# A decoder layer on one core: up and down units of its expert network in one line through all visits

## What is computed

```
x = layernorm(x + attention(x))              # 16 heads of 16, softmax, projections wq wk wv wo
x = layernorm(x + recurrence(x, ctx))        # a decaying scan over tokens, with exp(x) and exp(-x)
x = layernorm(x + experts(x))                # 8 experts, 256 -> 1024 -> 256, tanh GELU
```

```
h1  = gelu(x @ W1[e] + b1[e])
out = sum over e of gate[:, e] * (h1 @ W2[e] + b2[e])
```

## Time and profile before

| | |
|---|---|
| time, three executions | 1025.46, 1026.37, 1026.95 us (median 1026.37) |
| the profiled execution | 1025.53 us, span 1023.8 us |
| TensorE matmuls busy | 917.6 us (90%) |
| VectorE, ScalarE busy | 602.8 and 602.0 us (59% each) |
| GpSimd busy | 84.2 us (8%) |
| HBM traffic | 165 GB/s over the span |

### The profile page before, as it was taken

The page is one execution under the profiler, slowest core; times in us unless marked ns, Lnnn a source line. Parts: engine busy times, 40 slices in busy tenths (PEclk is TensorE's granted clock), DMA queues, the critical chain, the costliest instruction groups (busy, mean ns, idle before and its releaser), DMA issues.

```text
span 1023.8 us, 17885 instructions
## 1 busy us (share of the span) xinstructions
PE 917.6 (90%) x6672; PEld 824.0 (80%) x6672; DVE 602.8 (59%) x1254; ACT 602.0 (59%) x1017; POOL 84.2 (8%) x116
## 2 busy tenths in 40 slices
PE   4558697988799989999899989999899989999997
PEld 3457586778688879888788879888798888899997
DVE  6747667776565555565556645565556636333765
ACT  4437775666556655555556655555566645444685
POOL 3301001100020001100020001100011000000000
PEclk8667987999999999999999999999999999999999
DMA  6337879755554545454544455445454545565350
GB/s 208 102 126 258 278 251 316 255 198 179 172 168 142 157 140 173 128 173 135 160 150 150 139 167 156 150 149 158 134 167 128 164 141 158 175 195 155 118 171 11
DMA packets 143541, 170.33 MB, mean 166 GB/s; under 512 B 11080, under 2 KB 110688, under 8 KB 143456
## 3 DMA queue, kind: packets, MB, share of 16 engines
q1 hardware_dynamic: 143456, 169.19, 52.3%
HBM read 133.50 MB, written 35.65 MB: 165 GB/s over the span
## 4 chain that ended last, share of the span: by engine, by line
PE 72%; DVE 12%; ACT 11%; issue 3%; DMA 0%; POOL 0%; SPq 0%; POOLq 0%; ACTq 0%; DVEq 0%
PE up_ps L448 11%; PE up_ps L450 10%; PE up_ps L449 10%; PE down_ps L664 10%; PE down_ps L666 9%; PE down_ps L665 9%; ACT probs L717 2%; ACT L717 2%; DVE h_lo L830 2%; DVE pt_lo L905 2%; PE bank L487 2%; PE bank L448 2%; PE bank L470 1%; PE bank L450 1%; PE bank L449 1%
## 5 line engine op out<-in xcount | busy, mean ns | idle before, releaser
L768 ACT ACTIVATE h_all<-up_ps,b_all 128x512 f32<-128x512 f32 (+1 forms) x296 | 182.4, 631 | 344.3 <-PE up_ps L450 340.0
L664 PE MATMUL down_ps<-w_hi,h_hi 128*128 128x256 f32 x1024 | 300.6, 294 | 32.0 <-DVE h_lo L830 31.9
L665 PE MATMUL down_ps<-w_lo,h_hi 128*128 128x256 f32 x1024 | 292.3, 285 | 0.0
L666 PE MATMUL down_ps<-w_hi,h_lo 128*128 128x256 f32 x1024 | 292.3, 285 | 0.0
L830 DVE TENSOR_TENSOR h_lo<-h_all,h_hi 128x512 fp32r<-128x512 f32 x256 | 176.7, 692 | 191.8 <-ACT h_hi L759 190.7
L664 PEld LDWEIGHTS down_ps<-w_hi,h_hi 128*128 128x128 f32 x1024 | 198.0, 193 | 46.2 <-issue 32.4
L448 PE MATMUL up_ps<-x2t_hi,w_hi 128*128 128x512 f32 (+1 forms) x592 | 224.7, 380 | 0.9 <-DVE x2t_lo L830 0.9
L449 PE MATMUL up_ps<-x2t_lo,w_hi 128*128 128x512 f32 (+1 forms) x592 | 219.4, 371 | 0.0
L450 PE MATMUL up_ps<-x2t_hi,w_lo 128*128 128x512 f32 (+1 forms) x592 | 219.3, 370 | 0.0
L665 PEld LDWEIGHTS down_ps<-w_lo,h_hi 128*128 128x128 f32 x1024 | 198.6, 194 | 4.4
L666 PEld LDWEIGHTS down_ps<-w_hi,h_lo 128*128 128x128 f32 x1024 | 198.6, 194 | 0.0
(11 more groups left out here) (172 smaller groups left out, 1008.5 us busy)
## 6 DMA issues: line engine op xcount, KB each, us to landing
w_hi<-w_parts SPq DMA_DIRECT2D x192, 256.0 KB, 3.1
w_lo<-w_parts SPq DMA_DIRECT2D x192, 256.0 KB, 3.4
w_raw<-in_w_dram SPq DMA_DIRECT2D x104, 256.0 KB, 3.8
w_parts<-w_hi SPq DMA_DIRECT2D x64, 256.0 KB, 3.7
w_parts<-w_lo SPq DMA_DIRECT2D x64, 256.0 KB, 4.1
x_in<-in_x_dram SPq DMA_DIRECT2D x8, 256.0 KB, 3.8
ctx_sb<-in_ctx_dram SPq DMA_DIRECT2D x8, 256.0 KB, 4.3
out_dram<-acc SPq DMA_DIRECT2D x8, 256.0 KB, 2.4
```

What stands on the lines that cost most here:

```text
L664: nc.tensor.matmul(ps, hi, w2h[:, c, :], start=c == 0 and j == 0, stop=False, skip_group_check=True)
L665: nc.tensor.matmul(ps, hi, w2l[:, c, :], start=False, stop=False, skip_group_check=True)
L666: mm = nc.tensor.matmul(ps, lo, w2h[:, c, :], start=False, stop=c == FC - 1 and j == PAIR - 1, skip_group_check=True)
L768: a = nc.scalar.activation(h_all[:, unit % HALL, k * wide:(k + 1) * wide], up_ps[unit % 2][:, k * wide:(k + 1) * wide], ACT.Gelu_apprx_tan ...
```

## The change

The units are put in one line through all visits, by `plan()`. After each up unit comes the down unit three behind it; the first down unit of a visit comes one up unit later, together with the second. A two-pair visit's items (after another two-pair visit) are now

```diff
-    def items(n):
-
-        m = units(n)
-        order = [("U", u) for u in range(LAG)]
-        for u in range(LAG, m):
-            order += [("D", u - LAG), ("U", u)]
-        return order + [("D", u) for u in range(m - LAG, m)]
+    def plan():
+        ups = [(n, u) for n in range(VISITS) for u in range(units(n))]
+        lines, downs = [[] for _ in range(VISITS)], 0
+        for g, (n, u) in enumerate(ups):
+            lines[n].append(("U", n, u))
+            while downs + LAG + (ups[downs][1] == 0) <= g:
+                lines[n].append(("D",) + ups[downs])
+                downs += 1
+        return lines[:-1] + [lines[-1] + [("D",) + unit for unit in ups[downs:]]]
+
+    ITEMS = plan()
+    LINE = [item for line in ITEMS for item in line]
+    LAST_DOWN = [max(i for i, (kind, m, _) in enumerate(LINE) if kind == "D" and m == n) for n in range(VISITS)]
...
+    def up_before(i):
+
+        return [LINE[i - 1][1:]] if i > 0 and LINE[i - 1][0] == "U" else []
+
+    def ended(i):
+
+        return [(n, [p for p in range(NPAIR) if n == JOIN[p] + E - 1]) for n in range(VISITS - 1) if LAST_DOWN[n] == i]
...
             def down(n, u):
 
                 unit = FIRST_UNIT[n] + u
-                if u == 0 and n > 0:
-                    pe.wait_ge(added, EVACUATED[n])
...
                     for a in range(pairs):
+                        if c == 0 and n > 0 and a < len(active(n - 1)):
+                            pe.wait_ge(added, EVACUATED[n - 1] + PAIR * (a + 1))
...
             for n in range(VISITS):
-                order = items(n)
-                for k, (kind, u) in enumerate(order):
-                    if k > 0 and order[k - 1][0] == "U":
-                        hidden_hi(n, order[k - 1][1])
+                for k, (kind, visit, u) in enumerate(ITEMS[n]):
+                    for unit in up_before(FIRST_ITEM[n] + k):
+                        hidden_hi(*unit)
                     if kind == "U":
-                        hidden(n, u)
-                    if n == 0:
-                        for part in FIRST_ROUTE.get(k, []):
-                            route(0, part)
+                        hidden(visit, u)
+                    for part in FIRST_ROUTE.get(FIRST_ITEM[n] + k, []):
+                        route(0, part)
...
-                for k, (kind, u) in enumerate(order):
-                    if k == 0 and n > 0:
-                        add_expert(n - 1)
+                for k in range(len(ITEMS[n])):
+                    for done, left in ended(FIRST_ITEM[n] + k - 1):
+                        add_expert(done)
                         for p in left:
                             finish(p, 0)
-                    if k > 0 and order[k - 1][0] == "U":
-                        hidden_lo(n, order[k - 1][1])
...
+                    for unit in up_before(FIRST_ITEM[n] + k):
+                        hidden_lo(*unit)
...
-BEGIN = (None, 0, 40, 88, 152, 216, 280, 344, 408)
-LENGTH = (None, 40, 48, 64, 64, 64, 64, 64, 64)
+BEGIN = (None, 0, 36, 85, 149, 213, 277, 341, 405)
+LENGTH = (None, 36, 49, 64, 64, 64, 64, 64, 64)
...
-NORM3_ITEM, STORE_ITEM = 2, 4
...
+NORM3_AFTER, STORE_AFTER = 3, 5
+FIRST_PIECES = [(0, 0, 0), (0, 0, 1), (0, 0, 2), (0, 0, 3), (0, 1, 0), (0, 1, 1), (0, 1, 2)]
+FREE_FIRST = {0: [(0, 1, 3)], 1: [(1, 0, 0)], 2: [(1, 0, 1)], 3: [(1, 0, 2)]}
+FREE = [[{0: [(0, 0, 3)], 1: [(1, 0, 0)], 2: [(0, 1, 0)], 3: [(0, 1, 1)], 4: [(1, 0, 1)], 5: [(0, 1, 2)], 6: [(1, 0, 2)],
+          7: [(0, 1, 3)]},
+         {0: [(0, 0, 3)], 2: [(0, 1, 0)], 3: [(0, 1, 1)], 4: [(1, 0, 0)], 5: [(0, 1, 2)], 7: [(0, 1, 3)], 8: [(1, 0, 1)],
+          11: [(1, 1, 0)], 12: [(1, 0, 2)], 15: [(1, 1, 1)], 16: [(1, 0, 3)]}],
+        [{1: [(1, 0, 0)], 2: [(0, 1, 2)], 3: [(1, 0, 1)], 5: [(1, 0, 2)], 6: [(0, 1, 3)]},
+         {2: [(0, 1, 2)], 3: [(1, 0, 0)], 6: [(0, 1, 3)], 7: [(1, 0, 1)], 10: [(1, 1, 0)], 11: [(1, 0, 2)], 14: [(1, 1, 1)],
+          15: [(1, 0, 3)]}]]
```

More of the change, by code:

```diff
@@ L55, in units, with table @@
         return FC if len(active(n)) == 2 else G
-    def items(n):
-        m = units(n)
-        order = [("U", u) for u in range(LAG)]
-        for u in range(LAG, m):
-            order += [("D", u - LAG), ("U", u)]
-        return order + [("D", u) for u in range(m - LAG, m)]
+    def plan():
[10 more added lines that the diff above has]
+    LAST_DOWN = [max(i for i, (kind, m, _) in enumerate(LINE) if kind == "D" and m == n) for n in range(VISITS)]
+    def table(n):
+        if n == 0:
+            return FREE_FIRST
+        return FREE[len(active(n - 1)) - 1][len(active(n)) - 1]
     def splits(n, k):
-        table = SPLIT_TWO if len(active(n)) == 2 else SPLIT_ONE
-        return [(n + d, i, q) for d, i, q in table.get(k, []) if n + d < VISITS and n + d not in KEPT]
+        return [(n + d, i, q) for d, i, q in table(n).get(k, []) if n + d < VISITS and n + d not in KEPT]
     def loads(n, k):
-        table = LOAD_TWO if len(active(n)) == 2 else LOAD_ONE
-        return [(n + d, i, q) for d, i, q in table.get(k, []) if n + d in KEPT]
+        return [(n + d, i, q) for d, i, q in table(n).get(k, []) if n + d in KEPT]
+    def up_before(i):
+        return [LINE[i - 1][1:]] if i > 0 and LINE[i - 1][0] == "U" else []
+    def ended(i):
+        return [(n, [p for p in range(NPAIR) if n == JOIN[p] + E - 1]) for n in range(VISITS - 1) if LAST_DOWN[n] == i]
     FIRST_UNIT = list(itertools.accumulate((units(n) for n in range(VISITS)), initial=0))
-    FIRST_ITEM = list(itertools.accumulate((len(items(n)) for n in range(VISITS)), initial=0))
+    FIRST_ITEM = list(itertools.accumulate((len(line) for line in ITEMS), initial=0))
+    PIECES = FIRST_PIECES + [piece for n in range(VISITS) for k in range(len(ITEMS[n])) for piece in splits(n, k)]
     EVACUATED = list(itertools.accumulate((PAIR * len(active(n)) for n in range(VISITS)), initial=0))
@@ L212, in sequence @@
         def sequence(n, i, q):
-            return 2 * G * turn_of(n) + ORDER.index((i, q))
+            return PIECES.index((n, i, q))
         def by_chunk(t):
@@ L364, in load_piece @@
             def load_piece(m):
[L365 to L368, removed]
+                if m >= len(PIECES):
                     return
-                i, q = ORDER[j]
+                n, i, q = PIECES[m]
                 if m >= RAW:
-                    before, was = divmod(m - RAW, 2 * G)
-                    which, part = ORDER[was]
-                    sp.wait_ge((w1_ready, w2_ready)[which], G * before + part + 1)
+                    before, which, part = PIECES[m - RAW]
+                    sp.wait_ge((w1_ready, w2_ready)[which], G * turn_of(before) + part + 1)
                 if i == 0:
@@ L416, in _ @@
             load_ctx(1)
-            for m in range(2 * G - 1):
+            for m in range(len(FIRST_PIECES)):
                 load_piece(m + RAW)
-            for m in range(2 * G - 1):
-                keep(0, *ORDER[m])
+            for first_piece in FIRST_PIECES:
+                keep(*first_piece)
             for n in range(VISITS):
-                for k in range(len(items(n))):
+                for k in range(len(ITEMS[n])):
                     for visit, i, q in splits(n, k):
@@ L435, in _ @@
                             load_ctx(p + 1)
[L436 to L439, removed]
+                    for _, left in ended(FIRST_ITEM[n] + k - STORE_AFTER):
+                        for p in left:
+                            store(p)
             store(NPAIR - 1)
@@ L675, in _ @@
             for n in range(VISITS):
-                for k, (kind, u) in enumerate(items(n)):
+                for k, (kind, visit, u) in enumerate(ITEMS[n]):
                     if kind == "U":
-                        up(n, u)
+                        up(visit, u)
                     else:
-                        down(n, u)
-                    if n == 0:
-                        for part in FIRST_ROUTE.get(k, []):
-                            route(0, part)
+                        down(visit, u)
+                    for part in FIRST_ROUTE.get(FIRST_ITEM[n] + k, []):
+                        route(0, part)
                     for p, s in steps(FIRST_ITEM[n] + k):
@@ L1091, in _ @@
                         split_lo(visit, i, q)
-                    if k == NORM3_ITEM:
+                    for _, left in ended(FIRST_ITEM[n] + k - NORM3_AFTER):
                         for p in left:
@@ L1165, in _ @@
             for n in range(VISITS):
[L1166 to L1170, removed]
+                for k in range(len(ITEMS[n])):
+                    for _, left in ended(FIRST_ITEM[n] + k - 1):
+                        for p in left:
+                            finish(p)
                     for p, s in steps(FIRST_ITEM[n] + k):
```

21 lines of the change are left out of this document (6 added, 15 removed).

## The result

The changed kernel takes **1041.36 us** (four executions, 1041.1 to 1044.46) where the kernel before took 1026.53 us beside it (four, 1025.46 to 1026.95): ratio 1.0153, 95% interval 1.0132 to 1.0174. It is slower, as forecast, by 15 us where 20.5 were forecast. The profiled execution has a span of 1039.9 us, 16.1 us more than before.

What follows compares the result with a forecast made beforehand. TensorE, busy 90% of the span, was taken as the bound. In visits 8 to 27, 46.75 us of new waits for 26.3 gave +20.5; with -1 and +1 elsewhere, 1026.4 + 20.5 made 1047 us, range 1012 to 1060.

Steps and rivals of the forecast that it cites:

- h_lo waits removed: Visits 8 to 27: down units at visit borders no longer wait for h_lo on TensorE; 25.5 us gone.
- values behind pt_lo: Visits 8 to 27: a table load and GELU delay pt_hi, so value products wait 3.3 and 1.9 us; 26 us.
- back transposes behind exp_k: Visits 8 to 27: VectorE's scans start behind h_lo of U7, so BACK waits 2.15 us a block; 10.75 us.
- scores behind probs: Visits 8 to 27: VectorE does h_lo before neg_max, so second scores wait 0.55 us, twice a block; 5.5 us.
- gates: Route part 3 stands behind U7's GELU and a load, so part 4's transposes wait 0.75 us six times; 4.5 us.
- clock: Visits 8 to 27: fifteen waits of about 2 us and more might lower TensorE's clock; 0 to 15 us, taken as 0.
- visits 0 to 7: Opening visits: removed h_lo and pt_lo waits against new delays sum to -1 us, bounds -9 and +12.
- visits 28 to 36: End: in visits 33 to 36 D0 waits some 0.3 us four times behind add_expert; +1 us.
- The split wait of down(): New waits of down(), one for each pair's two adds, cost 0 because U3 and U4 (2.8 us) cover them.
- Transfers: Kept weight loads, visits 8 to 31, are issued at least 12 items (17 us) before use: hidden, no cost.
- Nothing replaces the border waits: Rival: border waits go without new ones; 1001 us, up to 1020 with some new waits; chance 0.13.
- The rival of the low clock after each long wait: Rival: opening suffers, +12 us, or low clock after each long wait, +8 to +12; 1058 us, chance 0.15.

Runs made afterwards that it cites:

- pt_hi first: Changed kernel with, on ScalarE for pairs 3 to 7, a TURN step's pt_hi ahead of the same item's GELU: 1011.64 us, ratio 0.9856.
- earlier exponentials: Changed kernel with the exponentials of the second attention one step earlier (XEXP_STEP 43 for 44): 1030.51 us, ratio 1.006.
- five buffers: Changed kernel with five buffers of h_hi and h_lo for four (HALF = 5): 1036.45 us, ratio 1.009.
- before with the earlier exponentials: Kernel before the change, with the exponentials of the second attention one step earlier (XEXP_STEP 43 for 44): 1021.96 us, ratio 0.9963.
- value products later: Changed kernel with all four value products one item later, and TURN of the second and fourth with them: 1023.87 us, ratio 0.9965.
- gates later: Changed kernel with GATE at steps 1 and 3 for 0 and 3: 1032.41 us, ratio 1.0073.
- before with shifted steps: Kernel before the change, old order of units, with the attention of pairs 3 to 7 beginning two items earlier: 1054.7 us, ratio 1.0273.
- one wait: Changed kernel with a visit's first down unit waiting once for all adds of the visit before, not per pair: 1050.15 us, ratio 1.0241.
- all of them together: Changed kernel with pt_hi ahead of GELU, VALUE one item later, HALF = 5, XEXP at step 43, GATE one item later: 990.27 us, ratio 0.9656.
- no second table: Changed kernel with GELU's activation replaced by Tanh, which shares the exponentials' table; not the exact function: 982.47 us, ratio 0.9585.

## Why the prediction was right, and where it was off

**Sign and mechanism.** Slower, by ScalarE's order, as forecast: 1041.4 us, in the range, inside the forecast's own 1035 to 1054. The profile shows the four lines of waits that were named, and no others, in visits 8 to 27.

| term (visits 8 to 27 unless said) | forecast, us | measured, us |
|---|---|---|
| h_lo waits removed | -25.5 | -25.5 |
| values behind pt_lo | +26 | +22.4 |
| back transposes behind exp_k | +10.75 | +8.9 |
| scores behind probs | +5.5 | +3.5 |
| gates | +4.5 | +3.2, and 0.6 in visit 28 |
| idle time, sum against 26.3 | +20.5 | +11.7 |
| clock | 0 (0 to 15) | +6.3 |
| visits 0 to 7 | -1 | -3.5 |
| visits 28 to 36 | +1 | +1.6 |
| sum | +20.5 | +16.1 (span) |

**Values.** Right in kind: the experiment that puts pt_hi first removes 17.7 of the 22.4 us. Each product's wait was sized 0.36 us too long (3.3 and 1.9 us forecast, 2.94 and 1.54 measured, of which 0.15 each is that for the second half). A part of it is that one activation starts 0.1 us before the one ahead of it ends (pt_hi at 339.64 under a GELU that ends at 339.74), where the sum laid them end to end.

**Back transposes and scores.** inc_b to exp_k takes 7.9 us, from 374.27 to 382.13, as forecast (7.85); counted from inc_b, TensorE came to it 0.4 us later than forecast. The wait at the scores was 0.33 to 0.44 us where 0.55 was taken. The earlier exponentials remove the one line, and five buffers take away 2.6 of the 3.5 us of the other, so both causes are shown; the 0.9 us left are not explained.

**Clock.** This is the step of the sum that failed: "Fifteen waits of about 2 us and more will stand there", taken as 0 because "four of the five like it did not show it". That was a misreading of the trace of before, as its windows behind the five waits of 2.85 us tell (three of them):

```profile
373.30:376.70 3.40, 3.40 (x14) 3.28 (x15) 0.54 (x2) 0.39 (x1) 0.00 (x0) 0.50 0.00 2
...
724.90:728.30 3.40, 3.40 (x10) 2.72 (x10) 3.03 (x9) 0.47 (x1) 0.00 (x0) 0.50 0.49 154
840.90:844.30 3.40, 3.40 (x12) 2.85 (x11) 2.30 (x7) 0.00 (x0) 0.00 (x0) 0.51 0.32 96
```

The waits ended at 373.26, 723.47 and 839.91 us. In the last two cases the fall came 1.4 and 1.0 us after the wait's end, when D7, the one place that the prediction looked at, was done or nearly so. Three of five were followed by the low level, and ten new waits, five of them of 2.79 us, had to be expected to bring more. They did: six slow stretches in place of three, five behind the 2.79 us and one behind a 1.39 us wait, and 6.3 us more for the same matmuls. These filled most of the 8.8 us by which the waits fell short of the forecast: that the total came out closer than its parts is luck. The kernels with the same matmuls give a price, as busy time of visits 8 to 27 against the number of slow stretches in them: 0 and 552.4 us (pt_hi first), 0 and 552.7 (before with the earlier exponentials), 2 and 557.2 (value products later), 3 and 557.0 (before), 4 and 559.3 (gates later), 5 and 561.2 (five buffers), 6 and 563.3 (after), 7 and 567.6 (before with shifted steps), 9 and 570.5 (one wait). Against 552.5 us that is 1.5 to 2.4 us a stretch; 3.4 us at half the clock would lose 1.7 us, an estimate from the windows above. It is a rough price: the two kernels with the fewest waits have no slow stretch either, and 549.2 us (all of them together) and 547.6 (no second table). So some 3 to 5 us of the busy time follow something else than slow stretches, and what it is stays open.

**The split wait of down().** Valued at nothing, since U3 and U4 cover the adds. They nearly do (0.2 us are missed five times), but taking the split back costs 8.8 us, 7.2 of the 9.2 us in visits 8 to 27 as busy time. So the changed kernel came out well also because of an edit to which the forecast gave no worth; without it the time would have been 1050 us.

**Visits 0 to 7.** -3.5 for -1, inside the bounds given. Long waits have moved rather than gone: the one for acc in visit 7, 4.56 us at 261.31, is new. No experiment took this part alone.

**Transfers.** Hidden, as forecast: three items' delay changed nothing.

**The Trainium skill** ("ScalarE: Activation LUTs", rules for kernel authors) says to finish one table set before switching. The Tanh kernel bears it out: without the second set 59 us of the changed kernel's 1041 go. Its price for a switch, a load of 1.28 us with a drain of 1.38 us on top ("What ACT_TABLE_LOAD costs"), isn't borne out in its second part: in the timeline of the changed kernel the exponential ends at 337.74, the load runs from 337.76 to 339.04, and the GELU starts at 339.05. By the prediction's estimate from the page the ten products would have waited up to 28 us longer with a drain, and they didn't.

**The rivals.** "Nothing replaces the border waits" was wrong for this change, but it is what pt_hi alone makes of it: 1011.6 us, inside its 1001 to 1020. Its condition was stated rightly: pt_hi has to start where it did. The rival of the low clock after each long wait was right in kind, with 6.3 us where it had 8 to 12; its other half, a worse opening, did not come.

## What to carry to other kernels

When units of work are put into a new order and side steps keep their item numbers, go through the items of the engine that turns between two tables, and look at what now stands between a step and the one that feeds the bottleneck; a load and a GELU (1.9 us) between an exponential and a copy cost 30 us here, more than a third of it as busy time of the same matmuls, and one edit of ScalarE's order gave them back. Judge the new order only after the side steps are placed for it: the same line of units gave 1041 us as it was and 990 us with five such edits. And count a long wait of the matmul engine at more than its length, and look for the granted clock in the microseconds behind it, not at the next instruction alone.

## What the hardware showed that was not expected

- The granted clock behind a wait of TensorE does not follow the length of that wait alone. Counted over visits 8 to 27 of all traces, a slow stretch began within 2 us behind 33 of 35 waits of 2.8 us, three of five of 2.85 us (the kernel before), none of five of 2.40 us (before, with the exponentials earlier), none of 35 of 1.78 us (for exp_k), and 12 of 40 of 1.34 to 1.39 us (at the first value product, or at the third one moved later); of these the changed kernel has one of five, the kernel with one wait for the adds four of five. What decides stays open.
- An edit that changes the idle time by 0.7 us (exponentials earlier, in the kernel before) made visits 8 to 27 faster by 3.6 us, through 4.3 us less busy time of the same matmuls and no slow stretch in place of three.
- 62 table loads of 1.28 us, 79 us of ScalarE, which is busy 58% of the span, cost 59 us of the kernel's time, through what they make late: in visits 8 to 27 two thirds of it is idle time of TensorE and one third busy time of the same matmuls.
